# An attention block on one core: the row of maxima turned and stored one step earlier, and SP's transfers joined

## The chip, the cores and the metric

The kernel runs on one core of one Trainium2 chip. The metric is the device time of one execution in microseconds (us); lower is better. The time is that of one whole execution.

## The reference

Four sequences of 1024 tokens and 512 channels go through one conditioned attention block with 16 heads of 32 channels each:

```python
h = _sln(hidden, w, ln_g, ln_b, Wg, bg, Wb, bb)          # layer norm, gain and bias made from cond_1024
qkv = (h @ Wqkv.T + bqkv).reshape(B, N, num_heads, hd, 3)
q, k, v = (jnp.moveaxis(qkv[..., i], 2, 1) for i in range(3))
energy = jnp.einsum('bhqd,bhkd->bhqk', q, k)
att = jax.nn.softmax(energy, axis=-1) / D ** 0.5
out = jnp.einsum('bhqk,bhkd->bhqd', att, v)
out = jnp.moveaxis(out, 1, 2).reshape(B, N, D) @ Wp.T + bp
h1 = out + hidden
return _sln(h1, w, ln_g, ln_b, Wg, bg, Wb, bb) + h1
```

(The three lines that take q, k and v apart are put into one here.)

## The kernel before

Every engine runs a program of its own, written out by hand; semaphores alone order them. The order of the work is set by small tables of steps and by the order of the code, and every transfer is issued by SP, one after the other, except that GpSimd stores most tiles of the output.

**Heads, iterations, steps.** There are 64 heads (4 sequences of 16). The main loop has 16 iterations of four heads (`s` = 0 to 3), and each head has eight steps (`k` = 0 to 7), so that an iteration has steps 0 to 31. The number of a head is `u = 4 i + s`. Into the first eleven iterations the layer norm and the projections of later tiles are woven (`tiles`), into the iterations from the fifth on the output projection and the second norm (`outs`). Ahead of the loop stands a lead part that projects the first tiles, behind it a tail that finishes the last four pairs of tiles.

**What is done per head.** Scores are made twice. The first time (`a_item`, L660) TensorE writes them with the queries on the partitions into `ps_a`, two banks in turn, and VectorE takes the largest of each half row (`ring_item`, L1048), sixteen items a head. `max_negated` (L1065) makes `neg_max`, 128 partitions by 8. Item 16 of a head turns that tile into 8 rows of 128 (L654), in the same two banks; VectorE splits the rows into a high and a low part in `max_rows` (`ring_row`, L1055 and L1057), and SP copies the parts into rows 96 and 97 of `q_stack` (`store_row`, L387). The second time (`turned_scores`, L674) TensorE makes the scores with the keys on the partitions and the two rows of maxima in the product, ScalarE takes the exponent into `p` (L858), and TensorE multiplies by `v` into `ps_o` (`weighted`, L691) and sums into `ps_s` (`pair_sums`, L704), after GpSimd has added pairs (L1249). The first turned scores of a head come in the last step (`k` = 7) of the head before it and wait for both parts of its row (`row_in`).

**The ring.** The items of `ps_a` have positions 0 to 16 in each head. The function `ring_items` says which stand in which step; the first of a step comes ahead of its turned scores, the others between the two of them. An item may be written when the item two places ahead of it has been read (`a_used`).

**What SP issues.** In step 1 of a head it loads the stacks of the head three further on (`load_stacks`, L373 and L376): rows 0 to 31 of `q_stack` and of `k_stack` and so on in blocks of 32 rows of 4 KB. In step 4 it stores the output of the head before (`store_att`, L395) and loads `v` (L380), in step 6 it stores the row of maxima (L387), in step 7 the sums (`store_sums`, L403). Once an iteration, in the second head, it stores the reciprocals of the sums (`store_recips`, L409, step 10), and in step 12 it waits until they have landed (`rcp_out`) and loads two tiles of the attention's output (L414) and of their scales (`load_scale`, L423). In between it stores the projections (`store_rows`, L356, and `store_v`, L363).

Of the kernel before, what the change touches and what calls it, by code (L numbers as in the profile page):

```python
# [19 lines left out]
F32 = mybir.dt.float32  # L20
# [39 lines left out]
def conditioned_attention(nc, x, cond, ln_g, ln_b, Wg, bg, Wb, bb, Wqkv, bqkv, Wp, bp, out):  # L60
    B, N, D = x.shape
# [21 lines left out]
    rcp_d = nc.dram_tensor("rcp_scratch", [B, H, N], F32, kind="Internal").ap()  # L83
# [4 lines left out]
    rcp_heads = rcp_d.rearrange("b (c s) (p j) -> (b c) p s j", s=4, p=128)  # L88
    rcp_tiles = rcp_d.rearrange("b (c s) (t n) -> b t s c n", s=4, n=128)
# [4 lines left out]
    with ExitStack() as ctx:  # L94
# [161 lines left out]
        def ring_items(k):  # L256
# [3 lines left out]
            items = {4: [(8, 2, 0), (9, 2, 1)], 5: [(10, 1, 16), (11, 2, 2), (12, 2, 3)],  # L260
# [44 lines left out]
        def _(sp):  # L305
# [65 lines left out]
            def load_stacks(v, s):  # L371
                for row, part in ((0, 0), (1, 0), (2, 1)):
                    sp.dma_start(q_stack[row * HD:(row + 1) * HD, s, :].bitcast(F32),  # L373
                                 qk_heads[part, bass.ds(v, 1)].rearrange("a d n -> (a d) n")).then_inc(qk_in[s], 16)
                for row, part in ((0, 2), (1, 3), (2, 2)):
                    sp.dma_start(k_stack[row * HD:(row + 1) * HD, s, :].bitcast(F32),  # L376
                                 qk_heads[part, bass.ds(v, 1)].rearrange("a d n -> (a d) n")).then_inc(qk_in[s], 16)
# [12 lines left out]
            def store_att(v, s):  # L390

                slot = s % 2
                sp.wait_ge(o_taken, v + 1)
                for e in range(4):
                    sp.dma_start(att_heads[bass.ds(v, 1), e].rearrange("v d n -> (v d) n"),  # L395
                                 o_stage[HD * e:HD * e + HD, slot, 0:QW]).then_inc(att_out[slot], 16)

            def store_sums(v, s):
# [3 lines left out]
                for e in range(4):  # L402
                    sp.dma_start(sum_t[HD * e:HD * e + HD, s, :], o_stage[HD * e:HD * e + 1, slot, QW:2 * QW]  # L403
                                 ).then_inc(att_out[slot], 16)

            def store_recips(i):

                sp.wait_ge(rcp_done, i + 1)
                sp.dma_start(rcp_heads[bass.ds(i, 1)].rearrange("a p s j -> (a p) s j"), rcp_t[:]).then_inc(rcp_out, 16)  # L409
# [6 lines left out]
            def load_scale(pair, a):  # L416
# [5 lines left out]
                for s in range(4):  # L422
                    sp.dma_start(scale_t[32 * s:32 * s + 32, a],  # L423
                                 part[:, :, s].rearrange("b t c n -> (b t) c n").to_broadcast([32, DC, 128])
# [920 lines left out]
```

## Time and profile before

| | |
|---|---|
| median of 3 runs | 1540.1 us (1534.51 to 1549.79) |
| the profiled execution | 1545.36 us, its span 1543.7 us |
| busy share of the span | TensorE 90%, weight loads 58%, VectorE 60%, ScalarE 47%, GpSimd 67% |
| mean granted TensorE clock | 0.961 of full |
| transfers | 175.62 MB, mean 114 GB/s; SP's queue 40.0% of 16 engines |

The profiled execution is one execution, its span the time from the first to the last instruction. A line such as L660 is a line of the kernel.
### The profile page before, as it was taken

How to read it: one execution, taken by the hardware profiler on the slowest of the kernel's cores; microseconds unless marked ns; L12 is line 12 of the kernel's file. 1: busy time of each engine (PE TensorE's matmuls, PEld its weight loads, DVE VectorE, ACT ScalarE, POOL GpSimd, SP SyncE). 2: the span in 40 equal slices, each digit the busy share in tenths (PEclk: the TensorE clock that was granted, in tenths of full speed). 3: DMA queues.
4: the chain of work that ended last, by engine and by line, in shares of the span. 5: the costliest groups of instructions: out<-in, count | busy, mean ns of one | idle time of the engine just before them, and what ended most of it. 6: DMA issues, size and time to landing. Idle time of an engine off the chain costs nothing.

```text
span 1543.7 us, 35342 instructions
## 1 busy us (share of the span) xinstructions
PE 1388.2 (90%) x10804; PEld 888.2 (58%) x10804; DVE 927.3 (60%) x1633; ACT 718.3 (47%) x1370; POOL 1030.1 (67%) x779
## 2 busy tenths in 40 slices
PE   6998999999999999999999999999898989899543
PEld 4887656565656566666666666666454545454233
DVE  5336666666666565666666666656566656565045
ACT  4221555555555454444555555455455555556200
POOL 2442556565655677677868777757777777778757
PEclk9999999999999999999999999999999999999766
DMA  6567443343434535342544535353323232322232
GB/s 221 167 187 201 114 99 110 84 123 82 121 85 123 133 103 144 106 135 71 164 106 130 136 103 144 83 153 90 105 75 105 78 103 78 105 75 57 63 110 82
DMA packets 219737, 175.62 MB, mean 114 GB/s; under 512 B 106740, under 2 KB 189684, under 8 KB 219672
## 3 DMA queue, kind: packets, MB, share of 16 engines
q1 hardware_dynamic: 217368, 167.46, 40.0%
q0 software_dynamic: 2304, 7.34, 1.2%
q8 instruction: 35, 0.57, 0.2%
q14 instruction: 30, 0.25, 0.1%
HBM read 114.87 MB, written 59.05 MB: 113 GB/s over the span
## 4 chain that ended last, share of the span: by engine, by line
PE 55%; POOL 15%; issue 13%; SPq 6%; DMA 4%; DVE 4%; POOLq 2%; ACT 1%; DVEq 0%; ACTq 0%
PE ps_a L660 11%; PE ps_o L691 9%; PE ps_st L674 9%; POOL p L1249 8%; PE ps_w L572 7%; PE ps_w L625 6%; PE ps_s L704 6%; PE ps_st L625 3%; SPq L423 2%; DMA q_stack<-max_rows 2%; POOL y_t L1227 1%; POOL y_t L1229 1%; POOL oT_s L1203 1%; DVE half_max L1048 1%; POOLq L1172 1%
## 5 line engine op out<-in xcount | busy, mean ns | idle before, releaser
L1048 DVE TENSOR_REDUCE half_max<-ps_a 128x1 f32<-128x512 f32 x1024 | 670.7, 687 | 420.6 <-PE ps_a L660 410.4
L1249 POOL TENSOR_TENSOR p<-p 128x1024 f32<-128x1024 f32 x256 | 610.8, 2388 | 341.7 <-PE ps_o L691 341.1
L858 ACT ACTIVATE p<-ps_st 128x512 f32<-128x512 f32 x1024 | 573.4, 597 | 507.2 <-PE ps_st L674 489.6
L660 PE MATMUL ps_a<-k_stack,q_stack 96*128 96x512 f32 x1024 | 455.5, 446 | 27.0 <-DVEq L1060 14.9
L674 PE MATMUL ps_st<-q_stack,k_stack 98*128 98x512 f32 x1024 | 417.6, 409 | 34.5 <-DMA q_stack<-max_rows 24.3
L660 PEld LDWEIGHTS ps_a<-k_stack,q_stack 96*128 96x128 f32 x1024 | 194.7, 190 | 216.3 <-issue 99.9
L691 PE MATMUL ps_o<-p,v_head 128*32 128x256 f32 x4096 | 274.6, 387 | 0.0
L674 PEld LDWEIGHTS ps_st<-q_stack,k_stack 98*128 98x128 f32 x1024 | 195.9, 192 | 74.6 <-issue 24.9
L691 PEld LDWEIGHTS ps_o<-p,v_head 128*32 128x32 f32 x4096 | 134.5, 111 | 99.2 <-issue 6.3
L704 PE MATMUL ps_s<-p,root_s 128*1 128x256 f32 x2048 | 160.3, 385 | 11.9 <-POOL p L1249 11.8
L625 PEld LDWEIGHTS ps_w<-hT_s,wqkv_s 128*128 128x128 f32 x1056 | 143.2, 190 | 10.8
L625 PE MATMUL ps_w<-hT_s,wqkv_s 128*128 128x256 f32 x1056 | 145.4, 282 | 0.0
L704 PEld LDWEIGHTS ps_s<-p,root_s 128*1 128x1 f32 x2048 | 27.1, 81 | 105.8 <-issue 88.6
L572 PE MATMUL ps_w<-wqkv_s,hT_s 128*128 128x512 f32 x324 | 86.9, 394 | 0.0
L572 PE MATMUL ps_w<-wp_s,oT_s 128*128 128x512 f32 x288 | 78.8, 395 | 0.0
L572 PE MATMUL ps_a<-wp_s,oT_s 128*128 128x512 f32 x96 | 31.9, 505 | 43.7 <-POOL oT_s L1203 43.7
L572 PEld LDWEIGHTS ps_w<-wqkv_s,hT_s 128*128 128x128 f32 x324 | 60.9, 189 | 13.9
L572 PEld LDWEIGHTS ps_w<-wp_s,oT_s 128*128 128x128 f32 x288 | 54.4, 189 | 12.8
L625 PE MATMUL ps_st<-hT_s,wqkv_s 128*128 128x256 f32 x360 | 48.9, 296 | 7.8 <-DVE hT_s L964 7.8
L572 PEld LDWEIGHTS ps_a<-wp_s,oT_s 128*128 128x128 f32 x96 | 24.3, 258 | 51.8 <-POOL oT_s L1203 45.9
L1203 POOL TENSOR_TENSOR oT_s<-att_t,oT_s 128x512 fp32r<-128x512 f32 x32 | 43.6, 1364 | 14.3 <-ACT oT_s L834 13.8
L625 PEld LDWEIGHTS ps_st<-hT_s,wqkv_s 128*128 128x128 f32 x360 | 47.6, 205 | 9.5 <-DVE hT_s L964 9.1
(98 smaller groups left out, 971.3 us busy)
## 6 DMA issues: line engine op xcount, KB each, us to landing
qk_scratch<-qkT_s SPq DMA_DIRECT2D x108, 256.0 KB, 2.4
q_stack<-qk_scratch SPq DMA_DIRECT2D x192, 128.0 KB, 2.8
k_stack<-qk_scratch SPq DMA_DIRECT2D x192, 128.0 KB, 3.0
x_tile<-in_x SPq DMA_DIRECT2D x32, 256.0 KB, 5.0
gq_s<-gain_bias_scratch SPq DMA_DIRECT2D x16, 512.0 KB, 4.4
v_scratch<-v_parts SPq DMA_DIRECT2D x32, 256.0 KB, 3.2
v_head<-v_scratch SPq DMA_DIRECT2D x64, 128.0 KB, 2.1
att_scratch<-o_stage SPq DMA_DIRECT2D x256, 32.0 KB, 1.5
```

What stands on the lines that cost most here:

```text
L423: sp.dma_start(scale_t[32 * s:32 * s + 32, a], part[:, :, s].rearrange("b t c n -> (b t) c n").to_broadcast([32, DC, 128])).then_inc(scale ...
L572: mm = pe.matmul(dst, left[:, lp, c, :], right[:, rp, c, :], start=(n == 0), stop=(n == 11))
L625: mm = pe.matmul(bank[:, part * 256:(part + 1) * 256], wqkv_s[:, lp, w, d, chunk * 128:(chunk + 1) * 128], hT_s[:, rp, d, :], start=(n == ...
L660: pe.matmul(ps_a[:, parity, :], q_stack[0:96, s, t * 128:(t + 1) * 128], k_stack[0:96, s, half * 512:(half + 1) * 512], start=True, stop=T ...
L674: pe.matmul(ps_st[:, ST_BANK[2 * k + e], :], k_stack[0:98, s, k * 128:(k + 1) * 128], q_stack[0:98, s, e * 512:(e + 1) * 512], start=True, ...
L691: mm = pe.matmul(ps_o[HD * e:HD * e + HD, 0:QW], v_head[:, s, k, :], p32[:, k, e * QW:(e + 1) * QW], start=(k == 0), stop=(k == 7))
L704: mm = pe.matmul(ps_s[HD * e:HD * e + 1, 0:QW], root_s[:], p32[:, 2 * j + 1, e * QW:(e + 1) * QW], start=(j == 0), stop=(j == 3))
L858: nc.scalar.activation(p32[:, k, e * 512:(e + 1) * 512], ps_st[:, ST_BANK[2 * k + e], :], ACT.Exp).then_inc(exp_done, 1)
L1048: V.tensor_reduce(half_max[:, s % 2, item:item + 1], ps_a[:, parity, :], AX.X, ALU.max).then_inc(a_used, 1)
L1172: pool.drain()
L1203: G.tensor_tensor(oT_s[:, a, 1], att_t[:, a], oT_s[:, a, 0].bitcast(F32), ALU.subtract).then_inc(out_lo, 1)
L1249: G.tensor_tensor(p32[:, 2 * j + 1, :], p32[:, 2 * j, :], p32[:, 2 * j + 1, :], ALU.add).then_inc(pair_added, 1)
```

## The change

It has three parts. Item 16, the turning of `neg_max`, moves from the first place of step 5 to the last place of step 4, and `store_row` from step 6 to step 5. SP's transfers are joined: four instead of six for the stacks, where the first takes one block of 32 rows from DRAM twice over; one instead of four for the output of a head and for its sums; one instead of four for the scales of a tile. For this the reciprocals lie in DRAM in another order and are stored by four transfers instead of one. The counts of the semaphores follow.

```diff
-    rcp_d = nc.dram_tensor("rcp_scratch", [B, H, N], F32, kind="Internal").ap()
+    rcp_d = nc.dram_tensor("rcp_scratch", [B, N // 128, 4, DC, 128], F32, kind="Internal").ap()
...
-    rcp_heads = rcp_d.rearrange("b (c s) (p j) -> (b c) p s j", s=4, p=128)
-    rcp_tiles = rcp_d.rearrange("b (c s) (t n) -> b t s c n", s=4, n=128)
+    rcp_heads = rcp_d.rearrange("b t s c n -> s b c t n")
+    rcp_tiles = rcp_d.rearrange("b t s c n -> b t s (c n)")
...
-            items = {4: [(8, 2, 0), (9, 2, 1)], 5: [(10, 1, 16), (11, 2, 2), (12, 2, 3)],
+            items = {4: [(8, 2, 0), (9, 2, 1), (10, 1, 16)], 5: [(11, 2, 2), (12, 2, 3)],
...
             def load_stacks(v, s):
-                for row, part in ((0, 0), (1, 0), (2, 1)):
-                    sp.dma_start(q_stack[row * HD:(row + 1) * HD, s, :].bitcast(F32),
-                                 qk_heads[part, bass.ds(v, 1)].rearrange("a d n -> (a d) n")).then_inc(qk_in[s], 16)
-                for row, part in ((0, 2), (1, 3), (2, 2)):
-                    sp.dma_start(k_stack[row * HD:(row + 1) * HD, s, :].bitcast(F32),
-                                 qk_heads[part, bass.ds(v, 1)].rearrange("a d n -> (a d) n")).then_inc(qk_in[s], 16)
+                head = qk_heads[:, bass.ds(v, 1)].rearrange("w a d n -> w (a d) n")
+                sp.dma_start(q_stack[0:2 * HD, s, :].bitcast(F32),
+                             head[0:1].to_broadcast([2, HD, N])).then_inc(qk_in[s], 16)
+                sp.dma_start(q_stack[2 * HD:3 * HD, s, :].bitcast(F32), head[1]).then_inc(qk_in[s], 16)
+                sp.dma_start(k_stack[0:2 * HD, s, :].bitcast(F32), head[2:4]
+                             ).then_inc(qk_in[s], 16)
+                sp.dma_start(k_stack[2 * HD:3 * HD, s, :].bitcast(F32), head[2]).then_inc(qk_in[s], 16)
...
                 sp.wait_ge(o_taken, v + 1)
-                for e in range(4):
-                    sp.dma_start(att_heads[bass.ds(v, 1), e].rearrange("v d n -> (v d) n"),
-                                 o_stage[HD * e:HD * e + HD, slot, 0:QW]).then_inc(att_out[slot], 16)
+                sp.dma_start(att_heads[bass.ds(v, 1)].rearrange("v e d n -> (v e) d n"),
+                             o_stage[:, slot, 0:QW]).then_inc(att_out[slot], 16)
...
                 sp.wait_ge(s_taken, v + 1)
-                for e in range(4):
-                    sp.dma_start(sum_t[HD * e:HD * e + HD, s, :], o_stage[HD * e:HD * e + 1, slot, QW:2 * QW]
-                                 ).then_inc(att_out[slot], 16)
+                sp.dma_start(sum_t[:, s, :], o_stage[0:128:HD, slot, QW:2 * QW]
+                             ).then_inc(att_out[slot], 16)
...
                 sp.wait_ge(rcp_done, i + 1)
-                sp.dma_start(rcp_heads[bass.ds(i, 1)].rearrange("a p s j -> (a p) s j"), rcp_t[:]).then_inc(rcp_out, 16)
+                for s in range(4):
+                    part = rcp_heads[s, bass.ds(i // 4, 1), bass.ds(i % 4, 1)]
+                    sp.dma_start(part.rearrange("b c t n -> (b c t) n"), rcp_t[:, s, :]).then_inc(rcp_out, 16)
...
                 part = rcp_tiles[bass.ds(T // per, 1), bass.ds(T % per, 1)]
-                for s in range(4):
-                    sp.dma_start(scale_t[32 * s:32 * s + 32, a],
-                                 part[:, :, s].rearrange("b t c n -> (b t) c n").to_broadcast([32, DC, 128])
-                                 ).then_inc(scale_in[a], 16)
+                sp.dma_start(scale_t[:, a].rearrange("p c n -> p (c n)"), part.rearrange("b t (s o) m -> (b t s) o m", o=1
+                             ).to_broadcast([4, HD, DC * 128])).then_inc(scale_in[a], 16)
...
-                        if k == 6 and not (last and s == 3):
+                        if k == 5 and not (last and s == 3):
                             store_row(u + 1, (s + 1) % 4)
```

TensorE in the third head of the first iteration, fifth and sixth step, before; L660 is an item, L654 the turning, L674 turned scores, L625 a projection:

```order
144 L660 MATMUL ps_a<-k_stack,q_stack 128x512 [waits qk_in2,a_used]
145 L674 MATMUL ps_st<-q_stack,k_stack 128x512 [waits exp_done]
146 L660 MATMUL ps_a<-k_stack,q_stack 128x512 [waits a_used]
147 L674 MATMUL ps_st<-q_stack,k_stack 128x512 [waits exp_done]
148 L625 MATMUL ps_w<-hT_s,wqkv_s 128x256 [waits tile_ev]
149 L625 MATMUL ps_w<-hT_s,wqkv_s 128x256 x11
150 L654 MATMUL ps_a<-ident,neg_max 8x128 [waits max_chain,a_used]
151 L674 MATMUL ps_st<-q_stack,k_stack 128x512 [waits exp_done]
152 L660 MATMUL ps_a<-k_stack,q_stack 128x512 [waits a_used] x2
153 L674 MATMUL ps_st<-q_stack,k_stack 128x512 [waits exp_done]
```

The same place of the changed kernel, whose lines have numbers one lower:

```order
144 L659 MATMUL ps_a<-k_stack,q_stack 128x512 [waits qk_in2,a_used]
145 L673 MATMUL ps_st<-q_stack,k_stack 128x512 [waits exp_done]
146 L659 MATMUL ps_a<-k_stack,q_stack 128x512 [waits a_used]
147 L653 MATMUL ps_a<-ident,neg_max 8x128 [waits max_chain,a_used]
148 L673 MATMUL ps_st<-q_stack,k_stack 128x512 [waits exp_done]
149 L624 MATMUL ps_w<-hT_s,wqkv_s 128x256 [waits tile_ev]
150 L624 MATMUL ps_w<-hT_s,wqkv_s 128x256 x11
151 L659 MATMUL ps_a<-k_stack,q_stack 128x512 [waits a_used]
152 L673 MATMUL ps_st<-q_stack,k_stack 128x512 [waits exp_done]
153 L659 MATMUL ps_a<-k_stack,q_stack 128x512 [waits a_used]
154 L673 MATMUL ps_st<-q_stack,k_stack 128x512 [waits exp_done]
```

The turning now stands between the second item and the second turned scores of step 4, ahead of the projection; step 5 has two items and no turning.

SP in the third head of the first iteration, from its step 1 to its step 7, before:

```order
114 L373 DMA q_stack<-qk_scratch 32x1024 [waits st_ready]
115 L373 DMA q_stack<-qk_scratch 32x1024 x2
116 L376 DMA k_stack<-qk_scratch 32x1024 x3
117 L395 DMA att_scratch<-o_stage 32x256 [waits o_taken]
118 L395 DMA att_scratch<-o_stage 32x256 x3
119 L380 DMA v_head<-v_scratch 128x256 [waits pv_done]
120 L363 DMA v_scratch<-v_parts 128x16x32 [waits tile_ev]
121 L387 DMA q_stack<-max_rows 1x8x128 [waits max_chain]
122 L387 DMA q_stack<-max_rows 1x8x128
123 L403 DMA sum_t<-o_stage 32x1x8 [waits s_taken]
124 L403 DMA sum_t<-o_stage 32x1x8 x3
```

The same place of the changed kernel (L373 to L378 load the stacks, L388 stores the row):

```order
119 L373 DMA q_stack<-qk_scratch 64x1x1024 [waits st_ready]
120 L375 DMA q_stack<-qk_scratch 32x1024
121 L376 DMA k_stack<-qk_scratch 64x1x1024
122 L378 DMA k_stack<-qk_scratch 32x1024
123 L395 DMA att_scratch<-o_stage 4x32x256 [waits o_taken]
124 L381 DMA v_head<-v_scratch 128x256 [waits pv_done]
125 L388 DMA q_stack<-max_rows 1x8x128 [waits max_chain]
126 L388 DMA q_stack<-max_rows 1x8x128
127 L363 DMA v_scratch<-v_parts 128x16x32 [waits tile_ev]
128 L402 DMA sum_t<-o_stage 128x1x8 [waits s_taken]
```

The row is now stored ahead of the tile of v (L363). The shapes are those that are written: 64 rows for the joined loads of the stacks, and 4 blocks of 32 rows for the output of a head.

## Rows read from the trace of the kernel before

**Rows 1.** Waits of TensorE: line <- releaser: us in total, times, longest.

```profile
PE ps_a L572 <- POOL oT_s L1203: 43.7, 4, 21.1
PE ps_st L674 <- DMA q_stack<-max_rows: 24.3, 13, 3.3
PE ps_a L660 <- DVEq L1060: 14.9, 45, 0.5
```

**Rows 2.** Timeline, SP, second head of sixth iteration: start, us, line, transfer.

```profile
581.41 1.32 SPq L373 DMA_DIRECT2D q_stack<-qk_scratch  x3
...
584.55 0.41 SPq L409 DMA_DIRECT2D rcp_scratch<-rcp_t  x1
585.63 1.83 SPq L395 DMA_DIRECT2D att_scratch<-o_stage  x4
...
589.84 1.88 SPq L423 DMA_DIRECT2D scale_t<-rcp_scratch  x4
...
592.77 1.82 SPq L423 DMA_DIRECT2D scale_t<-rcp_scratch  x4
...
596.00 1.45 SPq L387 DMA_DIRECT2D q_stack<-max_rows  x2
597.49 2.48 SPq L403 DMA_DIRECT2D sum_t<-o_stage  x4
```

**Rows 3.** Timeline of TensorE at two stalls, idle before in brackets.

```profile
597.86 0.40 PE L660 MATMUL ps_a<-k_stack,q_stack 96*128 96x512 f32 x1
600.59 0.50 PE L674 MATMUL ps_st<-q_stack,k_stack 98*128 98x512 f32 x1 [2.33 <-DMA q_stack<-max_rows]
...
1262.73 0.50 PE L674 MATMUL ps_st<-q_stack,k_stack 98*128 98x512 f32 x1 [2.62 <-DMA q_stack<-max_rows]
```

**Rows 4.** Stretches after two stalls: length, PE busy, PEclk, DMA share, GB/s.

```profile
600.60:605.60 5.00, 5.00 (x32) 0.66 0.35 109
...
1111.10:1116.10 5.00, 4.96 (x29) 0.50 0.56 158
```

**Rows 5.** Timeline of TensorE, fifth and sixth step of one head.

```profile
614.81 0.40 PE L660 MATMUL ps_a<-k_stack,q_stack 96*128 96x512 f32 x1
...
616.66 0.27 PE L654 MATMUL ps_a<-ident,neg_max 128*8 128x128 f32 x1
...
617.01 0.40 PE L660 MATMUL ps_a<-k_stack,q_stack 96*128 96x512 f32 x1
617.68 0.50 PE L660 MATMUL ps_a<-k_stack,q_stack 96*128 96x512 f32 x1 [0.27 <-DVEq L1060]
```

**Rows 6.** Timeline of VectorE in the same stretch.

```profile
614.77 1.29 DVE L1048 TENSOR_REDUCE half_max<-ps_a 128x1 f32<-128x512 f32 x2 [0.32 <-PE ps_a L660]
616.97 0.28 DVE L1055 CAST max_rows<-ps_a 8x128 fp32r<-8x128 f32 x1 [0.91 <-PE ps_a L654]
617.28 0.28 DVE L1057 TENSOR_TENSOR max_rows<-ps_a,max_rows 8x128 fp32r<-8x128 f32 x1
```

**Rows 7.** Timeline of SP where little else ran.

```profile
1423.57 1.43 SPq L387 DMA_DIRECT2D q_stack<-max_rows  x2
```

**Rows 8.** DMA view, 1423.5 to 1425.8 us: packets that ran.

```profile
DMA packets 32, 0.01 MB, mean 4 GB/s; under 512 B 16, under 2 KB 32, under 8 KB 32
```

**Rows 9.** DMA view, 1445 to 1448 us: packets that ran.

```profile
DMA packets 192, 0.13 MB, mean 44 GB/s; under 512 B 64, under 2 KB 192, under 8 KB 192
```

**Rows 10.** DMA view, 1189.5 to 1194 us: GB/s by slice, packets, share.

```profile
GB/s 0 0 328 255 0 291 219 109 328 328 437 37 182 328 328 364 364 328 146 146 401 292 218 255 182 292 182 182 255 218 0 0 0 0 0 0 0 0 0 0
DMA packets 288, 0.79 MB, mean 175 GB/s; under 512 B 96, under 2 KB 96, under 8 KB 288
...
q1 hardware_dynamic: 288, 0.79, 66.1%
```

**Rows 11.** Timeline of SP, first loads of the stacks.

```profile
118.12 1.29 SPq L373 DMA_DIRECT2D q_stack<-qk_scratch  x3
```

**Rows 12.** Timeline of VectorE ahead of the first iteration.

```profile
129.07 0.69 DVE L921 BATCH_NORM_STATS2 bn_t<-x_tile 128x6 f32<-128x512 f32 x1 [2.29 <-DMA x_tile<-in_x]
```

More of the change, by code:

```diff
@@ L512, in iteration @@
                             load_gain(go_s, go_in, pair)
-                            sp.wait_ge(rcp_out, 16 * i + ONE)
+                            sp.wait_ge(rcp_out, 64 * i + ONE)
                             for a in range(2):
@@ L542, in _ @@
             for half in range(2):
-                sp.wait_ge(att_out[half], 256 * ITERS)
+                sp.wait_ge(att_out[half], 64 * ITERS)
             for a in range(2):
@@ L546, in _ @@
             store_recips(ITERS - 1)
-            sp.wait_ge(rcp_out, 16 * ITERS + ONE)
+            sp.wait_ge(rcp_out, 64 * ITERS + ONE)
             for a in range(2):
@@ L657, in a_item @@
                 if item == 0:
-                    pe.wait_ge(qk_in[s], 96 * g + 96)
+                    pe.wait_ge(qk_in[s], 64 * g + 64)
                 pe.matmul(ps_a[:, parity, :], q_stack[0:96, s, t * 128:(t + 1) * 128],
@@ L840, in take_out @@
                 if not (isinstance(v, int) and v < 2):
-                    act.wait_ge(att_out[s % 2], 128 * (v // 2))
+                    act.wait_ge(att_out[s % 2], 32 * (v // 2))
                 nc.scalar.activation(o_stage[:, s % 2, 0:QW], ps_o[:, 0:QW], ACT.Copy).then_inc(o_taken, 1)
@@ L988, in recips @@
                 for half in range(2):
-                    dve.wait_ge(att_out[half], 256 * (i + 1))
-                dve.wait_ge(rcp_out, 16 * i + ONE)
+                    dve.wait_ge(att_out[half], 64 * (i + 1))
+                dve.wait_ge(rcp_out, 64 * i + ONE)
                 V.reciprocal(rcp_t[:], sum_t[:]).then_inc(rcp_done, 1)
@@ L995, in out_norm @@
                 dve.wait_ge(att_in[a], 16 * pair + 16)
-                dve.wait_ge(scale_in[a], 64 * pair + 64)
+                dve.wait_ge(scale_in[a], 16 * pair + 16)
                 V.tensor_tensor(att_t[:, a], att_t[:, a], scale_t[:, a], ALU.mult).then_inc(out_normed, 1)
@@ L1196, in out_norm @@
                 pool.wait_ge(att_in[a], 16 * pair + 16)
-                pool.wait_ge(scale_in[a], 64 * pair + 64)
+                pool.wait_ge(scale_in[a], 16 * pair + 16)
                 G.tensor_tensor(att_t[:, a], att_t[:, a], scale_t[:, a], ALU.mult).then_inc(out_normed, 1)
```

## The prediction

> **What bounds the kernel now.** I read the busy shares first: TensorE is busy for 90% of the span and every other engine for 67% or less, so the time is TensorE's work and the holes in it. Next the waits of TensorE [rows 1]. The largest, 43.7 us, lies in the tail, on GpSimd, out of the change's reach. Then come 24.3 us in 13 waits for the row of maxima and 14.9 us in 45 for VectorE's handling of the turned rows, which the change is about. The timeline shows how the former arise. All but one of the 13 stand in the second head of an iteration, from the fifth iteration on, where SP is late: between 585.63 and 594.6 us it issues sixteen transfers in a row, eight of them scales of 0.47 us each, and comes to the row only at 596.00 [rows 2]. TensorE ran out of work at 598.3 (its item at 597.86 and 0.4 us) and got the row at 600.59; in the later iterations, which are without projections, the wait is 2.62 us [rows 3]. After seven of these twelve stalls TensorE's granted clock was at its lower level, 1.2 of 2.4 GHz, for a while: 0.66 over the 5 us after the stall of 2.33 us, that is 3.4 us at half speed and 1.7 us lost, and over the 5 us after the longest one, of 3.3 us, all at half, 2.5 us lost [rows 1, 4]. So the row costs 24.3 + 6 x 1.7 + 2.5 = 37 us today. That is the most that the change can win there.
>
> **The turning one step earlier.** Now the turning runs behind a projection without a wait, but the second item behind it has one: 0.67 us behind the item ahead of it, 0.27 us of it idle, because VectorE must first copy and subtract the row [rows 5, 6]. In the changed order the turning follows the item of 614.81 at once and needs the bank of the item before that, whose maximum VectorE takes from 614.77 to 615.42 (half of a pair of 1.29 us) [rows 6]. That item of 614.81 is over at 615.21, so the turning sits idle for 0.2 to 0.3 us: step 4 gets as much longer as step 5, where VectorE is long done with the row when its second item asks for it, gets shorter. In a head without a projection in step 4 the turning already waits for the same maximum, and nothing changes. So one wait takes the place of another of its size; I take -0.06 us in 48 heads, -3 us. The bounds are 0.4 x 48 = 19 us either way, one if the wait in step 5 stays too, the other if the new one is hidden. The row is ready 1.4 us sooner.
>
> **Fewer issues.** With the joined transfers SP saves 3 x 0.47 us on the output of a head, 6 x 0.47 us on the scales, 3 x 0.62 us on the sums and 2 x 0.43 us on the stacks, and spends 3 x 0.41 us more on the reciprocals [rows 2]. Ahead of the row that is 9 x 0.47 = 4.2 us, and the row would leave SP at about 592, when its data are ready, not at 596.00. If that were all, it would be there ahead of 598.3 even with the 4.6 us from issue to TensorE's start that it took this time, and all 37 us would be won.
>
> **What a joined transfer does to the DMA engines.** This is the step on which the forecast rests. In one quiet stretch the two parts of one row ran, each 8 pieces of 512 B: 32 packets, 16 of them data and 16 small ones, so each part ended on 8 engines only [rows 8]. In another, four blocks of 32 rows of the output ran: 128 packets of 1 KB and 64 small ones, so each block was on 16 engines [rows 9]. Six transfers of 32 rows of 4 KB gave 192 + 96, again 16 engines each [rows 10]. A transfer is thus spread by the count of its outermost dimension: 8 rows on 8 engines, 32 rows on 16. The joined loads have 64 rows on the side of the stack, but on the side of DRAM they begin with a dimension of two: the block taken twice for `q_stack`, two tensors for `k_stack`. No row shows a transfer whose two sides differ. From both ends: spread by the stack's side it runs on 16 engines and costs nothing, spread by what divides both sides it runs on 2. I take 2, because an engine must get an equal share of both sides, and the row with its 8 pieces is the nearest case [rows 8]. By the same count the output of a head, the sums and the scales go to 4 engines and the reciprocals to 8.
>
> The Trainium skill (DMA: Bandwidth & Descriptors, Rules for kernel authors) says this outright: a leading zero-stride broadcast of c copies confines the whole DMA to at most c engines. The same table advises joining many small transfers into a large one, which speaks for the change. By the first rule the sum is the one below, by the second that of the first rival; the trace agrees with the first for 8 and 32 rows and doesn't show two.
>
> **What two engines cost.** A 4 KB packet took 0.661 x 16 x 4.5 us / 192 = 0.25 us when all 16 engines pulled at once, and at the slices of 437 GB/s, 27 GB/s an engine, 0.15 us [rows 10]. Two engines alone are not held up by the others: 0.16 us. A joined load is 64 packets, 32 an engine, 5.1 us; two of them and the two loads left over, 4 more packets, are 10.9 us on each of two engines, where it was 12 packets, 1.9 us. The two engines also carry a share of nearly every other transfer, and what is issued later stands behind. The stacks themselves are needed a head later, so only what queues behind them costs.
>
> *Second head, iterations 5 to 11.* Loads issued from 581.41; in the quiet stretch the packets of a part had run 1.5 us after the start of its issue, from 1424.29 to 1425.8 [rows 7, 8]; the two engines are free at 581.4 + 1.5 + 10.9 = 594, the reciprocals behind them land at about 596. SP waits for those ahead of the first tile and its scales, so it goes on at 596, not at 588.6. Then the row stands behind two tiles (256 KB on 16 engines, 1.0 us each), two scales (128 packets of 2 KB on 4 engines, 32 x 0.08 = 2.6 us each) and two stores of projections (0.75 us each): 8.7 us. It is there at 596.3 + 1.5 + 8.7 + 1.5 = 608, the last term an estimate for its own packets and their landing, against 598.3: a stall of 10 us, and the clock falls for longer than after 2.33 us, 2.7 us lost. 7 x 12.7 = 89 us.
>
> *Second head, iterations 12 to 15.* No store of projections, and the loads start some 2 us earlier against TensorE: 6.5 + 2.5 us, 4 x 9 = 36 us. *Iterations 1 to 4*, without scales: the row is about 1 us late, 4 us; in the last one, without stacks, 2 us. The other heads have at least 3 us to spare.
>
> *Lead.* Three heads of stacks from 118.12 on [rows 11], with the tile of x behind the first two. VectorE got that tile at 129.07 [rows 12]; with 21.8 us of loads on the two engines it gets it at 119.6 + 21.8 + 2.6 + 1 = 145, and the items of the ring wait behind: +16 us. *Tail.* Scales by one issue but on 4 engines, reciprocals by four issues: +3 us.
>
> **The sum.** 89 + 36 + 4 + 2 + 16 + 3 - 3 = 147 us, less the 37 us that these stalls replace: +110 us. On the profiled execution's 1545.4 us that is 1655; the median lies 5 us below, so 1650.
>
> **The rivals.** (1) *Sixteen engines after all.* The joined loads are spread by the stack's 64 rows, the row lands in time, the clock stays up: -37 - 3 + 3 = -37 us, some 1503 on the median. For it: the issue times, where SP is plainly late [rows 2]. Against it: the row on 8 engines [rows 8]. It is the case on the other side, and it decides at the number of engines: from about 8 on the loads of the stacks take under 3 us and are gone before the row. (2) *Two engines, but the row isn't held up by them,* because transfers of one queue overtake one another. Then only the lead and the wait for the reciprocals remain, 1515 to 1590. Against it: from the start of the second part's issue to TensorE's start it took 3.9 us where much stood ahead of it [rows 2, 3], though its packets need 1.5 us in quiet [rows 7, 8]. (3) *Worse:* packets of 0.25 us even on two engines, a burst of 17 us, 6 us more in each of the 11 second heads and stalls in the third heads too: above 1710. (4) *The turning's new wait brings the clock down* without any long stall, at 1.7 us a time; from 22 heads on that alone eats the gain of rival 1. The stalls of half a microsecond in step 5 did not do it, so I only widen by it.
>
> **How the numbers follow.** The forecast, 1590 to 1710, has 0.60; rival 1 has 0.16, rival 2 0.12, rival 3 0.12. A measurement of this kernel can't tell less than 1% from no change. Faster by more: rival 1 and a quarter of rival 2, 0.19; within 1%: 0.05; slower: 0.76. The range from 1530 to 1740 leaves out rival 1 and the far end of rival 3.
>
> **What would show it.** In the profile after: the landing time of the stacks' loads, some 6 us or more at the median; idle of TensorE before L673 released by the row, some 100 us in 11 to 20 waits; SP waiting for the reciprocals ahead of the tiles; granted clock at half after each second head; VectorE waiting for the tile of x at about 130 us. If the loads land in 3 us, the step on the engines is wrong and rival 1 holds. If step 4 shows a wait at L653 of about 0.5 us and the wait at L659 for VectorE's queue is gone, the part on the turning is right.

## The result

The changed kernel takes 1749.6 us (median of 4 runs, 1745.9 to 1754.4), the kernel before 1542.6 us beside it: a ratio of 1.1345, interval 1.128 to 1.141. The profiled execution has a span of 1745.0 us, against 1543.7 us before. Forecast were 1650 us, with a range of 1530 to 1740 us: slower, as forecast, and with the joined loads of the stacks on two engines, as said, but by 207 us where 110 were predicted.

The waits of TensorE after (line <- releaser: us in total, times, longest), to be read against [rows 1]. Lines are one lower than before:

```profile
PE ps_st L673 <- DMA q_stack<-max_rows: 147.7, 24, 13.3
PE ps_a L571 <- POOL oT_s L1202: 47.4, 4, 20.4
PE ps_a L653 <- DVE half_max L1047: 24.0, 62, 0.4
PE ps_s L703 <- POOL p L1248: 23.9, 12, 5.3
PE ps_a L659 <- DVE half_max L1047: 12.6, 7, 8.4
...
PE ps_a L659 <- DMA k_stack<-qk_scratch: 10.2, 1, 10.2
```

The row of maxima is now waited for 147.7 us instead of 24.3. The second head of the sixth iteration, the one of [rows 2, 3], shows how. SP's timeline (start, us, line, transfer), the counterpart of [rows 2]:

```profile
648.82 0.63 SPq L373 DMA_DIRECT2D q_stack<-qk_scratch  x1
...
652.24 5.25 SPq L410 DMA_DIRECT2D rcp_scratch<-rcp_t  x4
...
657.68 2.35 SPq L395 DMA_DIRECT2D att_scratch<-o_stage  x1
...
665.47 0.40 SPq L415 DMA_DIRECT2D att_t<-att_scratch  x1
...
669.90 1.50 SPq L388 DMA_DIRECT2D q_stack<-max_rows  x2
```

and TensorE's in the same stretch, the counterpart of [rows 3]:

```profile
665.33 0.40 PE L659 MATMUL ps_a<-k_stack,q_stack 96*128 96x512 f32 x1
677.30 0.79 PE L673 MATMUL ps_st<-q_stack,k_stack 98*128 98x512 f32 x1 [11.57 <-DMA q_stack<-max_rows]
```

SP begins the stacks' loads at 648.82, passes the wait for the reciprocals at 665.47, 16.7 us later (predicted 14.6), and TensorE gets the row 28.5 us behind the loads (predicted 26.6). While SP waits, the DMA engines are nearly idle at first. The DMA view of 657 to 667 us, in 40 slices (busy share in tenths, GB/s):

```profile
DMA  1101311110111113169412236979864211111044
GB/s 49 66 33 66 61 50 49 49 66 33 66 49 49 49 57 86 49 201 336 115 61 98 85 116 242 384 263 393 311 250 176 78 41 57 41 66 49 16 143 150
```

For the first four microseconds one to two sixteenths of the engines are busy, nearly all at 33 to 66 GB/s: two engines at some 25 GB/s each. The whole program's packets say the same (the pages of before and of after):

```profile
DMA packets 219737, 175.62 MB, mean 114 GB/s; under 512 B 106740, under 2 KB 189684, under 8 KB 219672
```

```profile
DMA packets 194262, 175.54 MB, mean 101 GB/s; under 512 B 93556, under 2 KB 160116, under 8 KB 194200
```

The scales by 2 KB in place of 512 B make 12288 packets fewer.
The clock after this stall (length, busy columns, then PEclk, DMA share, GB/s), the counterpart of [rows 4]:

```profile
677.30:682.30 5.00, 5.00 (x29) 2.37 (x30) 1.47 (x3) 1.19 (x2) 0.58 (x1) 0.50 0.22 74
682.30:687.30 5.00, 5.00 (x38) 3.29 (x36) 2.67 (x4) 2.28 (x4) 4.29 (x3) 0.85 0.36 104
```

Half speed for 6.5 us, 3.2 us lost. And in the lead, VectorE's tile of x [rows 12]:

```profile
148.84 0.69 DVE L920 BATCH_NORM_STATS2 bn_t<-x_tile 128x6 f32<-128x512 f32 x1 [10.53 <-DMA x_tile<-in_x]
```

### The profile page after: what moved, and what is told of

The parts are those of the page before. It is cut to its first block, busy times and chain, and to the rows that moved or that the text cites. A ratio compares the mean times of both kernels' runs of the same rounds, so it can differ in the third digit from the quotient of the medians.

```text
span 1745.0 us, 34256 instructions
## 1 busy us (share of the span) xinstructions
PE 1429.4 (82%) x10804; PEld 909.9 (52%) x10804; DVE 928.2 (53%) x1633; ACT 718.4 (41%) x1370; POOL 1028.1 (59%) x779
## 4 chain that ended last, share of the span: by engine, by line
PE 44%; issue 14%; POOL 13%; DMA 13%; SPq 8%; DVE 4%; POOLq 2%; ACT 1%; DVEq 0%; ACTq 0%
PE ps_a L659 9%; PE ps_st L673 8%; PE ps_o L690 7%; POOL p L1248 7%; PE ps_w L571 6%; DMA q_stack<-max_rows 6%; PE ps_s L703 5%; PE ps_w L624 5%; DMA rcp_scratch<-rcp_t 4%; PE ps_st L624 3%; SPq L410 2%; DVE half_max L1047 2%; POOL y_t L1226 1%; POOL y_t L1228 1%; SPq L395 1%
## 5 line engine op out<-in xcount | busy, mean ns | idle before, releaser
L673 PE MATMUL ps_st<-q_stack,k_stack 98*128 98x512 f32 x1024 | 430.3, 422 | 158.1 <-DMA q_stack<-max_rows 147.7
L673 PEld LDWEIGHTS ps_st<-q_stack,k_stack 98*128 98x128 f32 x1024 | 202.3, 198 | 201.7 <-issue 131.1
L659 PEld LDWEIGHTS ps_a<-k_stack,q_stack 96*128 96x128 f32 x1024 | 199.9, 196 | 201.6 <-issue 104.5
L690 PE MATMUL ps_o<-p,v_head 128*32 128x256 f32 x4096 | 287.5, 401 | 0.0
L690 PEld LDWEIGHTS ps_o<-p,v_head 128*32 128x32 f32 x4096 | 138.5, 115 | 109.5 <-issue 23.1
L703 PE MATMUL ps_s<-p,root_s 128*1 128x256 f32 x2048 | 167.4, 400 | 24.1 <-POOL p L1248 23.9
L1169 POOL TENSOR_TENSOR std_t<-mv_t,eps_s 128x1 f32<-128x1 f32 x32 | 6.0, 188 | 87.3 <-DVE mv_t L923 87.3
```

The source lines that it names most:

```text
L659: pe.matmul(ps_a[:, parity, :], q_stack[0:96, s, t * 128:(t + 1) * 128], k_stack[0:96, s, half * 512:(half + 1) * 512], start=True, stop=T ...
L673: pe.matmul(ps_st[:, ST_BANK[2 * k + e], :], k_stack[0:98, s, k * 128:(k + 1) * 128], q_stack[0:98, s, e * 512:(e + 1) * 512], start=True, ...
L690: mm = pe.matmul(ps_o[HD * e:HD * e + HD, 0:QW], v_head[:, s, k, :], p32[:, k, e * QW:(e + 1) * QW], start=(k == 0), stop=(k == 7))
L703: mm = pe.matmul(ps_s[HD * e:HD * e + 1, 0:QW], root_s[:], p32[:, 2 * j + 1, e * QW:(e + 1) * QW], start=(j == 0), stop=(j == 3))
```

## The experiments

Fifteen kernels. Times are medians, ratios are to the kernel before on the same chip.

**e1: the moved turning alone.** In the kernel before, item 16 goes to the end of step 4 and `store_row` to step 5.

> The kernel before with one part of the change alone: item 16 turned at the end of step 4 and the row stored in step 5; no transfer is joined. My theory (the added time comes from the joined loads of the stacks) expects a small gain: in the second heads SP is still late and only passes one or two stores of projections (0.75 us each) less ahead of the row, so each of its 11 late stalls of about 2 us gets some 0.8 us shorter: 1515 to 1540 us. The rival that the turning itself costs something (a new wait at L653 in every head, or the clock brought down by it) expects 1560 us or more.

1556.8 us, ratio 1.006 (1.004 to 1.008): neither. From the first head to the turning in the 44th the two kernels take 902.5 and 900.7 us; 12 us are lost from the twelfth iteration on, where GpSimd's sums come later and the clock falls:

```profile
1095.16 0.75 PE L704 MATMUL ps_s<-p,root_s 128*1 128x256 f32 x8 [2.27 <-POOL p L1249]
```

```profile
1095.16:1105.16 10.00, 9.85 (x76) 4.91 (x80) 5.52 (x10) 5.93 (x11) 7.01 (x3) 0.83 0.25 67
```

Before, this wait was 1.15 us and the clock stayed at full. e15 takes the row out of the comparison.

**e2: the stacks by six transfers.**

```diff
-                sp.dma_start(q_stack[0:2 * HD, s, :].bitcast(F32),
-                             head[0:1].to_broadcast([2, HD, N])).then_inc(qk_in[s], 16)
...
+                for row, part in ((0, 0), (1, 0), (2, 1)):
+                    sp.dma_start(q_stack[row * HD:(row + 1) * HD, s, :].bitcast(F32), ...
```

> The changed kernel with load_stacks as before, six transfers of 32 rows; everything else as changed. My theory expects nearly the whole slowdown to vanish: 1500 to 1530 us, row stalls under 25 us in sum, the x tile in the lead back at about 129 us. The rival that the other joined transfers (output, sums and scales on four engines, reciprocals by four issues) keep SP and the DMA engines busy expects 1620 us or more; both at work would give something between.

1629.4 us, ratio 1.054 (1.051 to 1.057): 120 us under the changed kernel, but 84 above the one before, so the stacks are not alone. The lead and iterations 1 to 4 are back at their old length, but twelve row stalls are left, 79.1 us:

```profile
1145.81 0.70 SPq L422 DMA_DIRECT2D scale_t<-rcp_scratch  x1
1146.67 1.63 SPq L387 DMA_DIRECT2D q_stack<-max_rows  x2
```

```profile
1157.29 0.79 PE L672 MATMUL ps_st<-q_stack,k_stack 98*128 98x512 f32 x1 [9.86 <-DMA q_stack<-max_rows]
```

The row is 10.6 us on the way behind two scales. The DMA view of 1152 to 1158 us shows four engines at work:

```profile
DMA  9998969898953222122222222223322222232231
GB/s 191 283 256 171 273 137 273 164 260 164 205 109 68 41 55 55 68 109 82 96 109 109 109 96 92 76 89 88 91 84 109 109 82 82 82 109 109 82 109 27
```

**e3: the same four loads, but of 64 rows that are neighbours in DRAM.**

```diff
-                             head[0:1].to_broadcast([2, HD, N])).then_inc(qk_in[s], 16)
+                two = [qk_shift[w, s % 2][bass.ds(v, 2)].rearrange("a d n -> (a d) n") for w in (1, 2)]
+                sp.dma_start(q_stack[0:2 * HD, s, :].bitcast(F32), two[0]).then_inc(qk_in[s], 16)
```

> The changed kernel, still with four loads of the stacks, of the same sizes and in the same places, but the two of 64 rows read 64 rows that lie one behind the other in DRAM (two neighbouring heads of one tensor), so that both sides have 64 as their outermost dimension. So the stacks hold other data, the two passes over the scores agree with each other, and the output is that of other scores. If it is the number of engines that costs (my theory), the loads are on 16 engines and the time is that of e2, within 10 us: 1500 to 1530 us. If it is the size of one transfer or the repeated or joined transfer as such, it stays at 1700 to 1750 us.

1627.8 us, ratio 1.053 (1.050 to 1.055), within 2 us of e2 (the 1500 to 1530 us erred with e2's). The size of a transfer and the number of issues play no part; the outermost dimension on the DRAM side does. That an outermost dimension of two confines a transfer to two engines is what the Trainium skill (DMA: Bandwidth & Descriptors, Rules for kernel authors) states, and the traces agree: e3 has 196054 packets, 1792 more than the changed kernel, which is exactly 16 small packets instead of 2 for each of two loads in 64 heads. The profile of e3 also gives the landing time of such a load, 3.6 us for 256 KB, where that of the changed kernel has none:

```profile
q_stack<-qk_scratch SPq DMA_DIRECT2D x64, 256.0 KB, 3.6
```

**e4: the joined stacks alone, in the kernel before.**

> The kernel before with the joined loads of the stacks alone. My theory expects the whole slowdown or more of it, since here SP still issues eight scales of 0.47 us ahead of a row that it stores a step later: 1720 to 1790 us. If the other joined transfers carry a good part of it, 1620 to 1700 us. If the stacks have nothing to do with it, 1540 us.

1746.9 us, ratio 1.128 (1.125 to 1.132): alone they cost nearly as much as the whole change. With e2 this shows that the costs don't add up: 202 us for the stacks alone, 84 for the rest alone (e2), 207 together. They overlap in the second heads, where both end in the wait for the row: of iterations 5 to 15 these take 86 us more than before in e4, 64 more in e2 and 111, not 150, more in the changed kernel. Outside them e4 costs more than the changed kernel: its row is waited for 41 times, 147.5 us in sum, many of them in other heads.

**e5: tiles and scales behind the row.**

```diff
-OUT_LOAD_STEP = 12
+OUT_LOAD_STEP = 14
```

> The kernel before with one number changed: SP waits for the reciprocals and loads the two tiles and their scales in step 14, behind the row of maxima, no longer in step 12, ahead of it. If what makes the row late is what SP issues and queues ahead of it in the second head (two tiles, eight scales), the row leaves SP some 3 us sooner and all 12 long row stalls go, with the clock they cost: 1505 to 1520 us. If the scales arrive too late for GpSimd, a wait at L1198 takes their place and the time stays within 1% of 1545 us.

1512.0 us, ratio 0.978 (0.975 to 0.981). No wait for the row is left, and no wait for the scales at L1198 has taken its place. The 33.6 us agree with the 37 us that the prediction had put on the row of the kernel before. This is the change's aim, by one number and without a joined transfer.

**e6: the same number in the changed kernel.**

> The changed kernel with the same one number changed, so that the joined loads of the stacks still run on two engines, but the row has neither the wait for the reciprocals nor the tiles and scales ahead of it. The prediction holds that the row is late because both come together: SP held by the reciprocals behind the burst, and then 8.7 us of tiles and scales. Then the second heads' stalls fall from 12 to 3 us or less each: 1590 to 1650 us. If the burst of the stacks by itself makes the row late, they stay at 8 us or more: above 1690 us.

1678.7 us, ratio 1.086 (1.081 to 1.091). Above the expected range: 71 us go, and 80.5 us of row waits are left, 32 of them. In iterations 5 to 11 the second head falls from 35.2 to 25.8 us on average, in the later ones to 17.4, but there the third head has a stall instead (27 us to the next turning where it was 18). So reciprocals, tiles and scales ahead of the row, taken together, are worth 9.3 of the 14.9 us that a second head of iterations 5 to 11 is longer than in e5, and the burst by itself 5.6.

**e7: scales and reciprocals as before, on top of e2.**

> As e2 (six loads of the stacks), and the scales and reciprocals too as before: eight transfers of the scales on 16 engines, one of the reciprocals. Left of the change are the moved turning, the output and the sums by one transfer each. e2 still had 12 stalls of 5 to 10 us in the second heads; my theory is now that they come from the joined scales, 64 packets of 2 KB on each of four engines ahead of the row. Then they go here: 1540 to 1560 us, as e1. If the joined output and sums on four engines hold the row up, it stays at 1600 to 1630 us.

1538.2 us, ratio 0.996 (0.994 to 0.998): the scales and reciprocals carry 91 us of e2. The output and the sums by one transfer on four engines are harmless; against e1 they win 19 us. SP is at the row 1.0 us sooner there (3.6 us after the turning instead of 4.6, mean of the second heads from the fifth iteration on), and the waits for the row fall from 23.0 to 14.1 us; they don't go.

**e8: the joined transfers alone, turning and row as before.**

> The changed kernel with the turning back in step 5 and the row stored in step 6: the joined transfers alone. The moved turning was worth +12 us in e1, which is 0.8% and came in the last iterations only. If the joins carry the slowdown, this kernel is within 15 us of the changed one: 1735 to 1765 us.

1763.5 us, ratio 1.143 (1.138 to 1.148). Where SP and the queue are late anyway, the turning and the row a step sooner are worth some 14 us by the medians; the intervals of the two ratios (1.138 to 1.148 here, 1.128 to 1.141 for the changed kernel) overlap a little, so the size is uncertain.

**e9: e5 with output and sums joined.**

> e5 (the kernel before with tiles and scales behind the row) and, of the change, only the output and the sums by one transfer each. In e7 against e1 these two were worth 18 us, all of it in row stalls. e5 has no row stall left, so if their gain is only the row's they are worth nothing here: 1505 to 1518 us, the time of e5. If they do something else as well (less load on the DMA engines, fewer small stalls), below 1500 us.

1508.8 us, ratio 0.976 (0.974 to 0.977): the fastest, and not to be told from e5. Where no row is late, fewer issues win nothing.

**e10 and e14: half a burst.** The changed kernel with only `k_stack`, or only `q_stack`, joined.

> The changed kernel with the three blocks of q_stack loaded one by one again, the first two of k_stack still joined: a burst of 64 packets on two engines for each head, half of the changed kernel's. If the stacks' cost grows with the burst beyond what is hidden, half a burst (5.1 us less in 12 second heads, some 10 us in the lead, little left in iterations 1 to 4) takes 70 to 110 us off 1750: 1640 to 1680 us, near e2's 1629. If one joined transfer alone is enough to hold up SP and the row, the time stays above 1700 us.

> The changed kernel with the three blocks of k_stack loaded one by one, the first two of q_stack joined (one block of DRAM taken twice): the mirror of e10 (1662 us). If a broadcast of two copies and two tensors both end on two engines, 1650 to 1675 us. If the one that is taken twice is spread otherwise, near e2's 1629 us or near 1700 us.

1662.4 us (ratio 1.076, 1.073 to 1.078) and 1676.6 us (1.085, 1.080 to 1.089; its profiled span, 1664.5 us, is 3 us above e10's). The second is just above its range. Both have 196182 packets, 1920 more than the changed kernel, 64 heads x 30: so a block taken twice and two tensors are both on two engines. They cost much the same; the intervals don't overlap, but what makes the 14 us between the medians wasn't tried. In both the lead is 10 us longer, and iterations 1 to 4 cost nothing (339.6 and 339.7 us against 338.9 in e5).

**e11: scales on 16 engines.** e2 with four transfers of 32 rows of 2 KB for a tile:

```diff
+                for s in range(4):
+                    sp.dma_start(scale_t[32 * s:32 * s + 32, a].rearrange("p c n -> p (c n)"),
+                                 part[:, :, s].rearrange("b t m -> (b t) m").to_broadcast([HD, DC * 128])
+                                 ).then_inc(scale_in[a], 16)
```

> e2 (1629 us: six loads of the stacks, the rest as changed) with the scales of a tile by four transfers of 32 rows of 2 KB, each on 16 engines, where e2 has one transfer of 128 rows on four; reciprocals and their place in DRAM stay as changed. If it is the four engines that make the row late, the cost of the scales goes although SP has six more issues of 0.47 us ahead of the row: 1530 to 1560 us, as e7 (1538). If it is the reciprocals' four stores or the wait for them, it stays at 1600 us or more.

1559.6 us, ratio 1.008 (1.006 to 1.011): 70 of e2's 91 us go with the engines alone, though SP issues more. The 21 us to e7, 16 of them in waits for the row (29.9 against 14.1 us), are left for the reciprocals: four stores, which hold SP up to 3.3 us instead of 0.4, and whatever their landing costs.

**e12: the lead's stacks by six.**

> The changed kernel with the three heads of stacks in the lead loaded by six transfers each; in the main loop nothing changes. The prediction put 16 us on the two-engine bursts in the lead, which delay the tile of x; the trace after has the lead 20 us longer. If these bursts are the cause, 1725 to 1735 us; if the lead is late for another reason (what the setup loads), 1745 to 1755 us.

1727.4 us, ratio 1.118 (1.115 to 1.120): the bursts in the lead cost 22 us.

**e13: the burst in two halves.**

```diff
-                            load_stacks(u + 3, (s + 3) % 4)
+                            load_q_stack(u + 3, (s + 3) % 4)
+                        if k == 3 and not (last and s > 0):
+                            sp.wait_ge(st_ready, 16 * u + 8)
+                            load_k_stack(u + 3, (s + 3) % 4)
```

> The changed kernel with each head's joined load of k_stack (and its third block) issued two steps later than that of q_stack, behind a wait for eight turned scores of the running head: the same transfers on the same two engines, but two bursts of 5 us some 5 us apart in place of one of 10.9 us. If what costs iterations 1 to 4 their 31 us is that SP is held in its issues while so much is queued for two engines, these iterations are back within 5 us of the kernel before and the joined output takes SP under 1 us to issue; in the second heads the reciprocals land sooner and the stalls fall from 12 to 3 to 7 us: 1630 to 1690 us in all. If the work on the two engines as such costs it, iterations 1 to 4 keep 15 to 31 us and the time stays above 1700 us.

1788.1 us, ratio 1.155 (1.151 to 1.159): the slowest of all; iterations 1 to 4 take 379 us where the changed kernel takes 370, though the output now takes SP 0.65 us on average. My theory of the hold-up, that SP's late issues are the cost, falls. It is true that SP is held while the burst runs. In the changed kernel, second head of the fourth iteration, the four stores of the reciprocals take 6.59 us and the joined output 2.19, and SP comes to a row that VectorE had finished at 469.5 only at 474.29:

```profile
461.93 6.59 SPq L410 DMA_DIRECT2D rcp_scratch<-rcp_t  x4
468.71 2.19 SPq L395 DMA_DIRECT2D att_scratch<-o_stage  x1
...
471.72 2.41 SPq L356 DMA_DIRECT2D qk_scratch<-qkT_s  x2
474.29 1.45 SPq L388 DMA_DIRECT2D q_stack<-max_rows  x2
```

```profile
469.19 0.28 DVE L1056 TENSOR_TENSOR max_rows<-ps_a,max_rows 8x128 fp32r<-8x128 f32 x1
```

```profile
478.48 0.50 PE L673 MATMUL ps_st<-q_stack,k_stack 98*128 98x512 f32 x1 [2.81 <-DMA q_stack<-max_rows]
```

In e13, same place, SP isn't held: the output takes 0.60 us, and the row, done at 479.2, is issued at 479.91. But it lands no sooner:

```profile
475.13 0.62 SPq L379 DMA_DIRECT2D k_stack<-qk_scratch  x1
...
476.42 0.60 SPq L402 DMA_DIRECT2D att_scratch<-o_stage  x1
...
479.91 2.07 SPq L395 DMA_DIRECT2D q_stack<-max_rows  x2
```

```profile
488.14 0.49 PE L683 MATMUL ps_st<-q_stack,k_stack 98*128 98x512 f32 x1 [2.72 <-DMA q_stack<-max_rows]
```

8.2 us from issue to TensorE, and 8.9 from VectorE's end, where the changed kernel has 9.0. My reading is that what counts is how much is still queued for the two engines when the row comes, whether SP waits for it in an issue or the row in the queue; the second half of the burst now stood right ahead of the row. With half a burst early in the head (e10, e14) the queue should be empty in time, and iterations 1 to 4 cost nothing.

**e15: e5 with the moved turning.**

> e5 (1512 us, without any row stall) with the turning moved to step 4 and the row stored in step 5. The prediction took -3 us for this part, with 19 us either way as bounds: 1505 to 1513 us. If the moved turning costs something by itself, as e1's +12 us had it, 1518 to 1526 us.

1517.7 us, ratio 0.981 (0.978 to 0.983), 5.7 us above e5, with intervals that overlap by a little. Four heads in a row take 79.92 us against 79.76 where nothing disturbs them, 0.2 us an iteration. The largest piece of the rest stands in the twelfth iteration, where TensorE waits 1.99 us behind GpSimd's sums instead of 0.80, the granted clock is 0.77 instead of 1.00, and 17.3 us between two turnings become 22.6. The turning moved to step 4 wins nothing by itself.

## Why the prediction was right and wrong

e5 is the kernel before without row stalls, so it is the base on which the prediction built its sum. The start of item 16 in each head, in the timeline, cuts the spans into stretches. From the turning in the second head of the sixth iteration, which stands ahead of the stall, to the next it is, in e5 and after,

```profile
591.72 0.27 PE L654 MATMUL ps_a<-ident,neg_max 128*8 128x128 f32 x1
...
611.98 0.27 PE L654 MATMUL ps_a<-ident,neg_max 128*8 128x128 f32 x1
```

```profile
658.54 0.27 PE L653 MATMUL ps_a<-ident,neg_max 128*8 128x128 f32 x1 [0.40 <-DVE half_max L1047]
...
693.67 0.27 PE L653 MATMUL ps_a<-ident,neg_max 128*8 128x128 f32 x1 [0.40 <-DVE half_max L1047]
```

so 20.26 and 35.13 us. Over the whole program:

| us | e5 | after | more | predicted |
|---|---|---|---|---|
| lead, to the turning in the first head | 168.8 | 187.6 | 18.8 (e12: 22) | 16 |
| iterations 1 to 4, to the turning in the second head of the fifth | 338.9 | 370.3 | 31.3 | 4 |
| second heads, iterations 5 to 11 | 7 x 20.25 | 7 x 35.16 | 104.4 | 89 |
| second heads, iterations 12 to 15 | 4 x 16.41 | 4 x 27.30 | 43.6 | 36 |
| all other heads up to the last iteration's second | | | 27.2 | 0 |
| behind that | 137.6 | 147.7 | 10.1 | 5 |
| the turning | | | within these | -3 |
| sum | 1509.6 | 1745.0 | 235.4 | 147 |

**Two engines.** Right, the step on which all rested: shown by the packets, and by e3. The landing time that was to show it can't be read, for the page gives none for these loads. The price of 0.16 us for a packet of 4 KB fits the 33 to 66 GB/s of two engines.

**The second heads.** Right in mechanism, some 15% short in size. The stalls of iterations 5 to 11 have a mean of 12.3 us (predicted 10), the clock after them costs 2.6 (predicted 2.7). SP passed the reciprocals 2 us later than predicted; their four stores had taken it 5.25 us where four of 0.41 were priced, but that this is the reason no run shows. That the wait for the reciprocals and the tiles with scales, taken together, stand between burst and row is shown by e6; e4 has stalls up to 11.6 us with the scales as before, and e2, e7 and e11 show that without a burst the scales on four engines make most of stalls of 5 to 10 us.

**"Iterations 1 to 4 ... the row is about 1 us late"** and **"The other heads have at least 3 us to spare"** are the steps that failed: 58 us where 4 stood, 54 of the error of 88. They failed for two different reasons.

In iterations 1 to 4 the row is late, and by more than 1 us: ten waits of 0.2 to 3.2 us, 19.1 us in sum, six of them outside the second heads, where 3 us were to be spare. I had let only the burst's 10.9 us stand ahead of the row and compared its end with the time at which the row is ready. But what SP has to issue between burst and row doesn't run ahead: it is held while the burst lasts, or queues behind it on the same two engines, and comes on top. In the fourth iteration the first load is issued at 458.77, the burst should be over at 471.2, and the row reaches TensorE at 478.48, 7.3 us later. Another 10.8 of the 31.3 us are the same matmuls at a lower granted clock. The stretch in e5 and after (length, busy time of TensorE, weight loads, VectorE, ScalarE and GpSimd, then PEclk, DMA share, GB/s):

```profile
168.83:507.77 338.94, 329.14 (x2748) 210.43 (x2745) 222.52 (x399) 181.55 (x349) 200.99 (x127) 1.00 0.39 103
```

```profile
187.60:557.90 370.30, 339.94 (x2746) 212.62 (x2746) 222.60 (x400) 182.04 (x350) 200.82 (x127) 0.97 0.32 92
```

With half a burst (e10, e14) this whole part is gone.

The 27 us in the later heads are not the row's: 22.9 of them stand in five stretches, from the turning in the first head to that in the second of iterations 12 to 16, and TensorE waits for no row there. It waits for GpSimd's sums, 17.4 us in ten waits where e5 has 6.0 in five, and is busy 11.2 us longer at a lower granted clock. The first of the five in e5, after and e10:

```profile
1068.88:1086.18 17.30, 16.02 (x130) 7.82 (x130) 11.24 (x21) 9.61 (x19) 13.99 (x9) 1.00 0.29 80
```

```profile
1227.74:1251.15 23.41, 19.40 (x130) 9.82 (x130) 11.53 (x21) 9.70 (x18) 18.09 (x11) 0.78 0.20 62
```

```profile
1151.40:1174.23 22.83, 19.25 (x129) 9.90 (x130) 11.53 (x21) 9.70 (x18) 17.56 (x11) 0.78 0.20 53
```

This cost doesn't shrink with the burst: against e5 the five stretches take 21.8 us more in e10 and 19.5 in e14, with half of it. In the eight kernels with a load of the stacks on two engines it is 16.8 to 22.9 us, in the others at most 9.5 (6.1 in e2, 7.9 in e3, 6.8 in e15). Ahead of each of the five in the changed kernel GpSimd sat idle for 2.9 to 3.8 us at L1172, where e5 has 0.2 to 1.1 us. So a load of the stacks on two engines reaches the loop by GpSimd too, a path that the prediction put at nothing; what GpSimd waits for there stays open.

Over the whole program TensorE is busy 1429.4 us for the same matmuls that take 1375.3 in e5. Of these 54 us, 26 are in the second heads of iterations 5 to 15, 10.8 in iterations 1 to 4 and 11.2 in the five stretches, all at a granted clock of 0.77 to 0.97 where e5 has 1.00.

**The old cost of the row.** Right: 37 us predicted, 33.6 won by e5.

**The turning.** The exchange of waits came as described, 24.0 us in 62 waits at L653, 0.39 us each, for 14.9 us in 45 at L660 and 2.5 in 15 for the turning's own (L654) in e5. The new one is the larger in sum, so the sign was wrong: some 6 us dearer (e15), inside the bounds given. Rival 4, the clock brought down by it alone, didn't come true in e15, whose mean granted clock is 0.964 against 0.969; the largest drop there goes with the longer wait behind GpSimd in the twelfth iteration.

**Fewer issues.** That nine issues fewer ahead of the row would bring it in time no run shows. e7 has three of the nine, those of the output: with them SP is at the row 1.0 us sooner and 19 us are won against e1, but 14.1 us of waits for the row are left.

**The rivals.** Rival 1 needed 16 engines, and e3 shows that the joined stacks get them only from other rows. (Its bound is a little off: by the prediction's own prices the loads on 8 engines take 3.2 us, not under 3.) Rival 2 is refuted by e13, where a row that is issued in time still lands 8.2 us later. Rival 3 is the side on which the time came, above 1710, and it named stalls beyond the second heads; but its reason, 0.25 us a packet, doesn't fit the two engines' rate, so that the time lies near it is no point for its mechanism.

## What to carry to other kernels

Before joining transfers, look at the outermost dimension on both sides. In this kernel 2 against 64 rows ended on 2 of 16 DMA engines, 4 on 4, and 64 against 64 on 16, as the packets count; two such loads a head on 2 engines cost 202 us against six small ones on 16 (e4). For a small urgent transfer ask what is queued ahead of it on any engine that it needs, and move that behind it: here one number in a table of steps won 2.2%, which all the joining had been for. When you price a queue, sum all that is issued between the large transfer and the urgent one; ends of bursts alone fall short. And don't end with the wait that you know: a quarter of the error, 22.9 of 88 us, came over another engine.

## What the runs showed of the hardware

- SP's issue of a transfer is itself held while few engines have much queued. The same joined output took SP 0.63 us to issue in e2, 0.88 and 1.23 us with half a burst (e10, e14), 1.93 us with the whole burst (after), 7.8 us at the longest (means over 64 issues from SP's timeline). So the issue times read from the kernel before were too low for the changed one.
- The bursts on few engines didn't add up here: 202, 84 and 207 us for one part, the other and both, since they meet in the row's wait of the second heads.
- GpSimd's short operation behind a `drain` (L1172) starts later in the eight kernels that have a load of the stacks on two engines: 27.0 (e4) to 49.9 us (e14) in 22 waits, 41.5 after. In the other nine it is 13.5 to 19.5 us, 16.7 before, also where the output, sums or scales are joined (e2, e3, e7, e9, e11). It doesn't follow the size of the burst, and what it waits for wasn't tried.
